# Top-2 choice, rank and scatter of tokens moved from a stage of their own into the attention loop, the last batch's output chain moved forward, the first experts' weights loaded earlier

## What is computed

```python
logits = h @ router_w.T                     # h = layernorm(x), 3584 x 8
vals, idx = lax.top_k(softmax(logits), 2)   # renormalised: vals / vals.sum()
for each expert e:                          # gate, up: 512 -> 352, down: 352 -> 512
    y = (silu(h @ gate_e.T) * (h @ up_e.T)) @ down_e.T
    out += combine[:, e] * y                # combine is zero where e was not chosen
```

## Time and profile before

| | us |
|---|---|
| median of three runs (1613.71 to 1620.02) | 1618.88 |
| profiled execution, its own time | 1616.73 |
| its span, first to last instruction | 1615.0 |
| PE busy, share of span | 1501.2, 93% |
| DVE busy, share | 899.4, 56% |
| POOL busy, share | 660.9, 41% |

### The profile page before, as it was taken

How to read it: one execution, slowest core, us unless ns; L and a number is a source line. 1 busy time by engine, 2 the same in 40 slices (tenths; PEclk the granted TensorE clock), 3 DMA queues, 4 the chain that set the end, 5 groups by cost and what they waited for, 6 DMA issues and landing times. The chain is left out here.

```text
span 1615.0 us, 40110 instructions
## 1 busy us (share of the span) xinstructions
PE 1501.2 (93%) x11594; PEld 1310.1 (81%) x11595; DVE 899.4 (56%) x2365; ACT 881.5 (55%) x2097; POOL 660.9 (41%) x671
## 2 busy tenths in 40 slices
PE   2899999999999999999999999983399999999896
PEld 2778888888888888888888888872299999999895
DVE  6557666766676667666776667654722222222221
ACT  2467667676767676676667667761033333333232
POOL 4233334333343234333333343323555555656453
PEclk9999999999999999999999999996599999999998
DMA  5567777677767776777677767763537766666643
GB/s 175 143 168 194 209 204 193 180 224 207 188 177 222 203 194 179 212 201 205 181 199 208 207 183 189 198 168 129 171 67 186 186 155 144 150 152 127 157 78 48
DMA packets 220125, 281.09 MB, mean 174 GB/s; under 512 B 83569, under 2 KB 164977, under 8 KB 220081
## 3 DMA queue, kind: packets, MB, share of 16 engines
q1 hardware_dynamic: 203952, 247.24, 54.4%
q0 software_dynamic: 16128, 33.30, 11.8%
HBM read 118.31 MB, written 66.17 MB: 114 GB/s over the span
## 5 line engine op out<-in xcount | busy, mean ns | idle before, releaser
L465 DVE CUSTOM_DVE_ANT_0 probs<-score,neg_mask 112x375 f32<-112x375 f32 x512 | 279.9, 547 | 262.2 <-PE score L555 260.7
L393 ACT ACTIVATE probs<-probs,neg_max 112x375 f32<-112x375 f32 x512 | 312.2, 610 | 185.8 <-DVE neg_max L465 183.3
L386 ACT ACTIVATE probs_t<-turn 125x336 f32<-125x336 f32 x512 | 225.0, 440 | 110.1 <-PE turn L563 110.1
L563 PE MATMUL turn<-ident,probs 112*125 112x112 f32 x1536 | 265.0, 281 | 2.9 <-ACT probs L393 2.9
L563 PEld LDWEIGHTS turn<-ident,probs 112*125 112x125 f32 x1536 | 222.7, 188 | 38.0 <-issue 14.1
L555 PE MATMUL score<-k_stack,q_stack 96*112 96x376 f32 x512 | 208.4, 407 | 5.9 <-DMA q_stack<-q_lo 5.5
L590 PE MATMUL proj<-ctx_hi,wk_hi 128*128 128x376 f32 x512 | 175.6, 343 | 1.9 <-PEq L29 1.1
L590 PE MATMUL proj<-ctx_hi,wk_lo 128*128 128x376 f32 x512 | 171.9, 336 | 0.0
L590 PE MATMUL proj<-ctx_lo,wk_hi 128*128 128x376 f32 x512 | 171.9, 336 | 0.0
L1031 DVE TENSOR_TENSOR a_lo<-a_ps,a_hi 128x384 fp32r<-128x384 f32 x63 | 35.1, 558 | 244.4 <-ACT a_hi L1006 244.4
L595 PE MATMUL proj<-wv_lo,ctx_hi 128*125 128x512 f32 x384 | 151.7, 395 | 0.0
(11 more groups left out here) (198 smaller groups left out, 3419.9 us busy)
## 6 DMA issues: line engine op xcount, KB each, us to landing
k_stack<-k_hi SPq DMA_DIRECT2D x512, 94.0 KB, 2.2
k_stack<-k_lo SPq DMA_DIRECT2D x256, 94.0 KB, 2.3
ctx_stage<-ctx_t SPq DMA_DIRECT2D x32, 750.0 KB, 5.3
q_stack<-q_hi SPq DMA_DIRECT2D x256, 56.0 KB, 2.0
w_raw<-gate_up_t SPq DMA_DIRECT2D x32, 352.0 KB, 3.1
gate_up_dram_hi<-w_hi SPq DMA_DIRECT2D x32, 352.0 KB, 5.5
gate_up_dram_lo<-w_lo SPq DMA_DIRECT2D x32, 352.0 KB, 5.9
gate_up_hi<-gate_up_dram_hi SPq DMA_DIRECT2D x16, 704.0 KB, 4.9
```

The costliest lines, as they stand in the source:

```text
L386: act.activation(probs_t[:, h % RING_T, :, :], turn[h % 2][0:LC, 0:LT * N].rearrange("p (l n) -> p l n", l=LT), ACT.Copy).then_inc(turned_ ...
L393: act.activation(probs[:, h % DS, :], probs[:, h % DS, :], ACT.Exp, bias=neg_max[:, par % 2, h:h + 1], scale=-1.0, accum_out=total[:, par ...
L465: dve.tensor_tensor_reduce(probs[:, h % DS, :], score[h % 2][0:N, 0:L], neg_mask[:, p, :], 1.0, BIG, ALU.add, ALU.min, neg_max[:, p, h:h + ...
L563: mm = pe.transpose(turn[h % 2][0:LC, l * N:(l + 1) * N], probs[:, h % DS, l * LC:(l + 1) * LC], W["ident"][0:N, 0:N])
```

## The change

- In pass `it`, for batch m2: DVE takes the logits from `misc` with a top-8 instruction (`max`) and an equality test in place of the copy to the list of all logits, and in ten further small steps (twelve in all, on at most 112 x 16 elements) finds the two experts as one-hot rows (lowest index first at a tie) and each token's slot. PE forms the rank in the batch with two bf16 products at step 11, into eight spare columns of the second score bank. POOL forms the shares (with one exponential on ACT) and issues two indirect scatters per pass, each of 112 entries of 8 bytes (token, share), into a DRAM table `slots`, where each expert has a region of 3584 slots.
- At the loop's end PE counts the tokens of each expert, and DVE makes the tile lists in 17 chained steps. The block `route` is gone. The table of slots, the padding rows and the constants are written in prepare_weights (three DMAs of 128 KB, two of 256 KB; 17 small POOL instructions behind its last one).
- The split of the experts' weights runs one pass earlier (for batch n in place of `it`), and SP issues the loads of experts 0 and 1 in pass 31, behind its x_res load. The expert buffers now lie in the whole program's memory, and the attention's wk, wv, context and k tiles lie in them; the loads wait until these are read.
- In pass 32 (`late`) the output chain of batch 31 is at steps 3 to 7 in place of 11 to 15, in two banks of its own (the free projection banks).
- In experts, POOL first gathers a tile's 128 entries from `slots`, then its rows by them; the share comes with the entry. The list copies and the gather of shares are gone; POOL's code is written out for all tiles in place of a loop.

The diff, cut to its core (removed: all of `route`):

```diff
+            for empty in slots.rearrange("(c p a) v -> c p (a v)", p=128, a=SLOTS):
+                sp.dma_start(empty, no_token[:, :, :].rearrange("p a v -> p (a v)")).then_inc(W["slots_cleared"], 16)
+            sp.wait_ge(zeroed, 1)
+            sp.dma_start(h2[T:T + PAD_ROWS, :], zero[:, :]).then_inc(W["pads_cleared"], 16)
+            sp.dma_start(pad_rows, zero[:, :]).then_inc(W["pads_cleared"], 16)
...
-                    need(sp, w_lo_made, it)
-                    sp.dma_start(w_raw[:, 0:WG], W["gate_up_flat"][:, bass.ds(it * WG, WG)]).then_inc(w_in, 16)
-                    sp.dma_start(w_raw[:, WG:WG + WD], W["down_flat"][:, bass.ds(it * WD, WD)]).then_inc(w_in, 16)
                 if has_n:
+                    need(sp, w_lo_made, n)
+                    sp.dma_start(w_raw[:, 0:WG], W["gate_up_flat"][:, bass.ds(n * WG, WG)]).then_inc(w_in, 16)
+                    sp.dma_start(w_raw[:, WG:WG + WD], W["down_flat"][:, bass.ds(n * WD, WD)]).then_inc(w_in, 16)
...
+                if has_n:
+                    need(sp, w_lo_made, n + 1)
...
+                if not inside and it == B - 1:
+                    sp.wait_ge(unit_out, UNITS * B)
+                    sp.wait_ge(w_stored, 64 * B)
+                    load_expert(sp, R, 0)
+                    for half in range(2):
+                        sp.wait_ge(k_stacked[half], 16 * KDMAS * B)
+                    load_expert(sp, R, 1)
...
+                if has_m2:
+                    need(pool, routed, ROUTE * m2 + 1)
+                    need(pool, grown_made, m2)
+                    pool.tensor_tensor(gap[:, :], ordered[:, 1:2], ordered[:, 0:1], ALU.subtract).then_inc(weighing, 1)
+                if has_n:
...
+                if has_n:
+                    need(pool, w_hi_made, n + 1)
+                    need(pool, w_stored, 64 * n)
...
+                if has_m2:
...
+                    need(pool, entered, 32 * m2)
+                    waited(pool)
+                    pool.tensor_copy(entry[:, :, 0], W["token"][:, 0:1].to_broadcast([N, 2])).then_inc(weighing, 1)
+                    need(pool, weighing, WEIGH * m2 + 2)
+                    waited(pool)
+                    pool.tensor_scalar(W["token"][:, :], W["token"][:, :], 1.0, float(N), ALU.mult, ALU.add).then_inc(weighing, 1)
+                    need(pool, grown_made, m2 + 1)
+                    waited(pool)
+                    pool.tensor_scalar(grown1[:, :], grown[:, :], 1.0, 1.0, ALU.mult, ALU.add).then_inc(weighing, 1)
+                    need(pool, weighing, WEIGH * m2 + 4)
+                    pool.tensor_tensor(entry[:, 0, 1:2].bitcast(F32), grown1[:, :], W["minus_one"][0:N, :], ALU.pow).then_inc(weighing, 1)
+                    need(pool, weighing, WEIGH * m2 + 5)
+                    pool.tensor_tensor(entry[:, 1, 1:2].bitcast(F32), grown[:, :], entry[:, 0, 1:2].bitcast(F32), ALU.mult).then_inc(weighing, 1)
+                    need(pool, weighing, WEIGH * m2 + 6)
+                    need(pool, routed, ROUTE * m2 + 10)
+                    waited(pool)
+                    for i in range(2):
+                        pool.indirect_dma_start(slots, bass.IndirectOffsetOnAxis(ap=at[:, i:i + 1], axis=0), entry[:, i, :], None).then_inc(entered, 16)
...
+                    if h == 12 and has_m2:
+                        need(act, weighing, WEIGH * m2 + 1)
+                        act.activation(grown[:, :], gap[:, :], ACT.Exp).then_inc(grown_made, 1)
+                    if h == 12 and has_n:
...
-                    if h == 5 and has_m2:
-                        need(dve, r_made, 2 * m2 + 2)
-                        dve.tensor_copy(W["logits"][0:N, bass.ds(m2, 1), :] if inside else W["logits"][0:N, m2:m2 + 1, :],
-                                        misc[0:N, 0:8].rearrange("p (a e) -> p a e", a=1)).then_inc(r_out, 1)
+                    if h == 11 and has_m2:
+                        need(dve, ranked, m2 + 1)
+                        dve.tensor_tensor(chosen[:, :, :], one[:, :, :], rank[0:N, :].unsqueeze(1).to_broadcast([N, 2, E]),
+                                          ALU.mult).then_inc(routed, 1)
...
+                    if h == 5 and has_m2:
+                        need(dve, r_made, 2 * m2 + 2)
+                        need(dve, weighing, WEIGH * (m2 - 1) + 1)
+                        waited(dve)
+                        dve.max(ordered[:, :], misc[0:N, 0:E]).then_inc(routed, 1)
+                        need(dve, routed, ROUTE * m2 + 1)
+                        dve.tensor_tensor(equal[:, :, :], misc[0:N, 0:E].unsqueeze(1).to_broadcast([N, 2, E]),
+                                          ordered[:, 0:2].unsqueeze(2).to_broadcast([N, 2, E]), ALU.is_equal).then_inc(r_out, 1)
+                    if h == 6 and has_m2:
+                        need(dve, r_out, 2 * m2 + 2)
+                        dve.tensor_tensor(weighed[:, :, :], equal[:, :, :], W["prio"][0:N, :].unsqueeze(1).to_broadcast([N, 2, E]),
+                                          ALU.mult).then_inc(routed, 1)
+                        need(dve, routed, ROUTE * m2 + 2)
+                        dve.tensor_reduce(best[0][:, :], weighed[:, 0, :], AX.X, ALU.max).then_inc(routed, 1)
+                    if h == 7 and has_m2:
+                        need(dve, routed, ROUTE * m2 + 3)
+                        dve.tensor_scalar(one[:, 0, :], W["prio"][0:N, :], best[0][:, 0:1], None, ALU.is_equal).then_inc(routed, 1)
+                        need(dve, routed, ROUTE * m2 + 4)
+                        dve.scalar_tensor_tensor(second[:, :], one[:, 0, :], -2.0 * E, weighed[:, 1, :], ALU.mult, ALU.add).then_inc(routed, 1)
+                        need(dve, routed, ROUTE * m2 + 5)
+                        dve.tensor_reduce(best[1][:, :], second[:, :], AX.X, ALU.max).then_inc(routed, 1)
                     if h == 6 and has_n:
...
+                    if h == 8 and has_m2:
+                        need(dve, routed, ROUTE * m2 + 6)
+                        dve.tensor_scalar(one[:, 1, :], W["prio"][0:N, :], best[1][:, 0:1], None, ALU.is_equal).then_inc(routed, 1)
+                        need(dve, routed, ROUTE * m2 + 7)
+                        need(dve, ranked, m2)
+                        dve.tensor_tensor(taken[0:N, :], one[:, 0, :], one[:, 1, :], ALU.add).then_inc(routed, 1)
+                    if h == 12 and has_m2:
+                        need(dve, routed, ROUTE * m2 + 9)
+                        need(dve, entered, 32 * m2)
+                        dve.tensor_reduce(at[:, :], chosen[:, :, :], AX.X, ALU.max).then_inc(routed, 1)
+                        dve.tensor_tensor(taken_sum[:, :], taken_sum[:, :], taken[0:N, :], ALU.add).then_inc(routed, 1)
                     if h == 10 and has_n:
                         need(dve, q_hi_made, n + 1)
...
-                    if h == 11 and has_m:
+                    if h == (3 if late else 11) and has_m:
+                        bank = o_bank if late else misc
...
-                    if h == 12 and has_m:
+                    if h == (4 if late else 12) and has_m:
...
-                    if h == 13 and has_m:
+                    if h == (6 if late else 13) and has_m:
...
+            def table(n, ins):
+                ins.then_inc(tabled, 1)
+                dve.wait_ge(tabled, n)
...
+            tile_no, tile_row = W["tile_no"], W["tile_row"]
+            dve.wait_ge(counted, 1)
...
+            table(4, dve.tensor_tensor_scan(last[:, :], W["ones"][:, :], tiles[:, :], 0.0, ALU.mult, ALU.add))
+            table(5, dve.tensor_scalar(jump[:, :], tiles[:, :], -float(SLOTS), float(region_rows(W["rows"])), ALU.mult, ALU.add))
+            table(6, dve.tensor_tensor(past, tile_no[:, :].unsqueeze(2).to_broadcast([128, NTP, E]),
+                                       last[:, :].unsqueeze(1).to_broadcast([128, NTP, E]), ALU.is_ge))
+            table(7, dve.tensor_reduce(expert[:, :], past, AX.X, ALU.add))
...
+            table(17, dve.tensor_copy(R["last"][:, :], last[:, :]))
...
+                    if h == 11 and has_m2:
+                        need(pe, routed, ROUTE * m2 + 8)
+                        if has_a:
+                            need(pe, masked, it * H + h - 1)
+                        pe.matmul(rank[0:N, :], W["before"][0:N + 1, 0:N], taken[0:N + 1, :], start=True, stop=False)
+                        pe.matmul(rank[0:N, :], W["ones16"][0:N, 0:N], taken_sum[:, :], start=False, stop=True).then_inc(ranked, 1)
                     if has_a:
+                        if h == 13 and has_m2:
+                            need(pe, routed, ROUTE * m2 + 9)
                         scores(it, par, h)
...
+                    if late and h == 3:
+                        need(pe, out_t_out, m + 1)
+                        turn_to_misc(lambda t: out_ts[:, t, :], W["ident"][:, :], o_bank, 128, N).then_inc(o_made, 1)
+                    if late and h == 6:
+                        need(pe, o_steps, 6 * m + 6)
```

(65 more changed lines are left out.)

346 lines of the change are left out of this document (107 added, 239 removed).

## The result

| | before | after |
|---|---|---|
| median time, us | 1618.59 | 1756.53 (1751.63 to 1760.88) |
| ratio | 1 | 1.0858, 95% interval 1.083 to 1.0887 |
| profiled span, us | 1615.0 | 1749.9 |
| two passes of the loop (one iteration, from DVE's branch back to the next, mean of twelve), us | 65.24 | 77.59 |

The account below looks back on a forecast made before the run. PE's own work was taken to bound the attention loop, PE hardly mattering in drain and route. Terms -29.7 + 3.0 - 0.3 + 6.2 + 5 + 2 = -13.8 gave 1602.9 profiled, 1605 us as median; range 1597 to 1623.

Parts of the forecast that it names:

- DVE's 12 steps (2.4 us a pass ...) lie in its idle time: Attention loop: DVE's added steps, 2.4 us a pass less one copy of 0.17, fit where DVE idles.
- PE's two products, +5: Attention loop: two more bf16 products on PE, 0.15 us a pass, +5 us in all, bounds 3 and 7.
- POOL's lateness, +2: Attention loop: entries and two scatters make x_s 0.9 us late; +2 us for passes in which slack is exceeded.
- rival 4: Loop: POOL's scatters stall it, 1633 us at 1.62 an issue, deciding from 1.35 an issue on; chance 0.16.
- The slack of 1.15: Loop: gaps of 0.33 before DVE's h_s and 0.80 behind h_t together take up 1.15 us of POOL's lateness.
- The rule on the shared ports: Loop: DVE in two-port mode blocks POOL's descriptor writes; a caught issue takes 1.5 for 0.95, +9 in all; not summed.
- The other meeting that I named: Loop, step 8: a product pair reading SBUF twice can meet POOL's q_tok; the next mask has two steps of room.
- Route, -29.7: Between last logits and experts: 38.74 us of route replaced by a 9.0 us chain for one batch, -29.7.
- the table ends the block: Block before the experts: DVE's table steps end last at 9.0 us, POOL's scatters having landed at 8.1.
- First tile, +3.0: Start of the experts: two dependent gathers, entries then rows, take 8.5 us against 5.46 from block's end to h_ps.
- Drain, +6.2: Last batches: experts' loads hold up batch 31's x_res, and POOL's fixed order makes x_s start at 1119.2, before 1113.05.
- The experts, -0.3: End of the experts: the copy of scatter_idx before the last scatter goes, -0.3 us.

Follow-up runs that it names:

- the increments: 20 semaphore increments of DVE, on which nobody waits, put ahead of the changed kernel's attention loop, nothing else: 1626.5 us.
- its copy with 20 increments: The kernel before with 20 semaphore increments of DVE put ahead of its attention loop: 1620.83 us, interval 1.0013 to 1.0047.
- the early DRAIN: Changed kernel, 20 increments, entries and scatters moved behind rstd except in the last two passes, plus one POOL DRAIN in the last pass: 1611.91 us, 0.9967.

## Why the prediction was wrong, step by step

- **The loop, "DVE's 12 steps (2.4 us a pass ...) lie in its idle time"**: this step failed. The time did lie there. What had no room was the number of instructions, which I never counted: 45 more in the two-pass body and 11 more ahead of it, with room for 7. The term was put at nothing and measured 130 us by the increments. None of the rivals had it either; the slower one ended at 1633 and by another way. Even without it the time lies above the range, by the terms below.
- **PE's two products, +5**: about right in size. Without POOL's lateness an iteration is 65.6 to 65.7 in the mean against 65.24, 0.2 a pass, 4 to 7 us in all. No run separates the products from the rest of the new work in that.
- **POOL's lateness, +2**: x_s was 0.85 late, as forecast (0.9; the terms as written add up to 0.7), and the issues cost 1.04 and 0.95, so rival 4's condition (1.35) was not met. The slack of 1.15 was read off the wrong follower. I asked who waits for h_s and not what is queued behind it. k_lo had no such room: 0.43 a pass by PE's waits, and 16 us in all by the iterations (66.89 to 65.69 over 13). The rule on the shared ports, which spoke against this part, was not put to the test here: the scatters' issues had ended 3.7 us before h_s began. The other meeting that I named did take place, `taken` with POOL's q_tok, in 29 of 32 passes, and cost PE nothing that its waits show.
- **Route, -29.7**: DVE's part measured 8.7 us from the last max to the last table step, against 9.0. POOL's scatters had landed 7.9 after it, against 8.1 (the terms as written add up to 7.45). But the block ended 4.6 us behind the table, with POOL's DRAIN, so "the table ends the block" was wrong. The sum of route and first tile is 21.2 in place of 17.5 (44.2 before). Without the scatters it is 16.9, with the early DRAIN 16.6.
- **First tile, +3.0**: from the DRAIN's end (1164.23) to h_ps (1172.09) it is 7.9 against 8.5, so +2.4.
- **Drain, +6.2**: x_s of batch 31 stands 6.6 further from that of batch 29, and the likeness of the two numbers is luck. The named mechanism exists (x_res landed 6.3 to 12.3 us after its issue with the loads ahead, 4.1 behind them), but it acts only behind x_s of batch 30, and there the distance grew by 1.7, from 15.1 to 16.8 (14.9 to 15.5 in copies of the old kernel that differ in nothing but increments; 18.2 in the changed kernel as it stands). The other 4.9 lie ahead of batch 30, where the same copies of the old kernel have 25.2 to 27.2 against 23.1 in the one profiled, and the run with 20 increments 28.0. There PE's clock is at 1.2 GHz for 3 us in the old kernel as it stood, for 14 in its copy with 20 increments and for 20 in the changed one with 20. Most of the 4.9 can come from that; I can't divide it further.
- **The experts, -0.3**: +0.5 to +8 in single profiles, open as told above.

## What to carry to other kernels

Before adding instructions to a hardware loop or ahead of it, count them for each engine, with waits and register work, and see where the body begins and ends in the packets of code; the engine that is 68% busy can be the one that is full. For DVE here, place and length together had to stay within 384. If instruction packets recur in a loop and an engine waits for "issue" at each branch back, move the body by some idle instructions before believing anything else of the profile. Where an operation gets later, read what is queued behind it, not only who waits for it.

## What the runs showed of the hardware

- A DVE loop body of 264 instructions that ended with its third packet of 128 took 65.29 us an iteration and no fetch; one that ended an instruction further took 74.54 and five fetches. Where a target was within 7 instructions of its packet's end, a second wait followed (2.4 to 4.9 us, behind a first of 5.6 to 7.2, from the second iteration on); at place 81 there was none. In all 7.6 to 11.3 us an iteration.
- POOL's DRAIN after 62 to 64 scatters took 5.3 to 5.8 us; with none before it 0.05, and with an early one before it 0.31. At the kernel's end it took 4.28 in the old kernel, 4.87 in the changed one and 2.50 with 59 small gathers fewer, so gathers count too.
- A DVE operation on two SBUF operands beside a long one of POOL (q_tok): `taken` took 1.24 us in 29 passes of 32, as long as q_tok ran, and 0.17 in the three without it. It was DVE that waited.
